# VectorE normalises all eight first tiles, GpSimd issues the weights between its powers, and the first and last attention chunk score their band units ahead of the products

## The reference

```
x = x + LN(attention(LN(x)))        # Wq, Wk, Wv 1024x1024 with biases, 16 heads of 64
x = x + LN(ffn(LN(x)))              # silu(x Wg') * (x Wu'), then Wd'; hidden 3072, int weights / 127
```

## Time and profile before

| | before |
|---|---|
| median of 3 runs | 1608.07 us (the fastest 1606.91) |
| the profiled execution | 1608.83 us, span of its slowest core 1607.8 us |
| spans of the 8 cores | 1602.8 to 1607.8 us |
| TensorE busy | 1551.7 us, 97% of the span |
| VectorE, ScalarE, GpSimd busy | 46%, 28%, 18% |
| chain that ended last | TensorE 94% |
| 0 to 10, 10 to 20, 20 to 30, 30 to 40, 40 to 50 us: TensorE busy | 0, 1.0, 2.5, 5.4, 7.7 us |
| 86 to 150 us (chunk 0): TensorE busy | 61.8 of 64 us |
| 562 to 640 us (most of chunk 7, and the FFN's start): TensorE busy | 70.5 of 78 us |
| 680 to 1608 us (FFN): TensorE busy | 920.5 of 928 us |

### The profile page before, as it was taken

How to read it: one execution, slowest core, us unless ns; L and a number is a source line. 1 busy time by engine, 2 the same in 40 slices (tenths; PEclk the granted TensorE clock), 3 DMA queues, 4 the chain that set the end, 5 groups by cost and what they waited for, 6 DMA issues and landing times.

```text
span 1607.8 us, 26300 instructions; the slowest of 8 cores (1602.8 to 1607.8 us)
## 1 busy us (share of the span) xinstructions
PE 1551.7 (97%) x9440; PEld 768.7 (48%) x9440; DVE 734.5 (46%) x1329; ACT 455.6 (28%) x566; POOL 293.8 (18%) x804
## 2 busy tenths in 40 slices
PE   2999999999999989999999999999999999999998
PEld 1455555555555554444444444444444444444443
DVE  3166555757565546424434434434434434433113
ACT  2445555555555551101111111111111111111111
POOL 3023323334332343200000001001001001001000
PEclk9999999999999999999999999999999999999999
DMA  9446756697664486932332333323322332322002
GB/s 222 92 76 129 144 101 119 139 155 151 135 114 97 91 243 220 246 110 85 92 99 98 92 86 111 93 85 111 88 77 97 85 95 92 92 79 95 10 1 92
DMA packets 130496, 178.41 MB, mean 111 GB/s; under 512 B 65472, under 2 KB 97216, under 8 KB 128960
## 3 DMA queue, kind: packets, MB, share of 16 engines
q1 hardware_dynamic: 110912, 99.11, 25.0%
q0 software_dynamic: 19024, 77.08, 19.4%
q10 hardware_dynamic: 432, 0.53, 0.1%
HBM read 136.85 MB, written 69.21 MB: 128 GB/s over the span
## 4 chain that ended last, share of the span: by engine, by line
PE 94%; DVE 1%; issue 1%; ACT 1%; POOL 1%; DMA 1%; DVEq 0%; POOLq 0%; SPq 0%; ACTq 0%
PE ps L655 21%; PE ps L665 21%; PE ps L721 20%; PE ps L293 14%; PE ps L323 7%; PE ps L368 4%; PE ps L394 3%; PE ps L391 2%; PE ps L418 1%; PE ps L440 1%; PE ps L623 1%; DMA xst<-x_in 0%; ACT pb L374 0%; DMA wdb_d<-wdT 0%; PE ps L263 0%
## 5 line engine op out<-in xcount | busy, mean ns | idle before, releaser
L655 PE MATMUL ps<-x2T,wg_sb 128*128 128x512 bf16 x1536 | 362.8, 379 | 1.2 <-DVE gacc L427 1.2
L665 PE MATMUL ps<-x2T,wu_sb 128*128 128x512 bf16 x1536 | 362.9, 379 | 0.0
L721 PE MATMUL ps<-wd_sb,hsw 128*128 128x512 bf16 x1488 | 322.5, 379 | 0.0
L374 ACT ACTIVATE pb<-ps 128x1024 bf16<-128x1024 f32 (+2 forms) x256 | 243.2, 1005 | 244.1 <-PE ps L368 244.1
L671 DVE TENSOR_TENSOR hsw<-ps,sgb 128x512 bf16<-128x512 f32 x192 | 132.8, 692 | 310.6 <-PE ps L665 310.6
L669 ACT ACTIVATE sgb<-ps 128x512 bf16<-128x512 f32 x192 | 114.6, 597 | 509.1 <-PE ps L655 497.4
L655 PEld LDWEIGHTS ps<-x2T,wg_sb 128*128 128x128 bf16 x1536 | 150.2, 98 | 181.9 <-issue 1.3
L665 PEld LDWEIGHTS ps<-x2T,wu_sb 128*128 128x128 bf16 x1536 | 150.2, 98 | 180.8
L721 PEld LDWEIGHTS ps<-wd_sb,hsw 128*128 128x128 bf16 x1488 | 145.6, 98 | 175.6
L172 POOL TENSOR_TENSOR small<-small 128x1 f32<-128x1 f32 x127 | 74.6, 588 | 742.6 <-DVE small L170 737.1
L381 POOL MEMSET pb<- 64x128 bf16 x488 | 111.7, 229 | 309.7 <-ACT pb L374 250.0
(11 more groups left out here) (80 smaller groups left out, 1093.4 us busy)
## 6 DMA issues: line engine op xcount, KB each, us to landing
xx<-x_in SPq DMA_DIRECT2D x34, 512.0 KB, 6.1
attn<-attn_d SPq DMA_DIRECT2D x32, 512.0 KB, 4.8
x_d<-xx POOLq DMA_DIRECT2D x32, 512.0 KB, 7.4
x1r<-x_d SPq DMA_DIRECT2D x32, 512.0 KB, 3.3
out<-x1r POOLq DMA_DIRECT2D x31, 512.0 KB, 3.0
xst<-x_in SPq DMA_DIRECT2D x29, 512.0 KB, 5.0
attn_d<-ast SPq DMA_DIRECT2D x58, 256.0 KB, 3.9
wgb_d<-wgT POOLq DMA_DIRECT2D x24, 256.0 KB, 5.7
```

Of the source, the lines that this page charges most:

```text
L374: s_free[buf] = tok["p", c, u, i] = AC.sig(ac.activation(pu[:, :, lo:hi], sp.rearrange("p (h e) -> p h e", h=2)[:, :, lo:hi], AF.Exp))
L655: mm = te.matmul(gp[:, p2], wg_sb[:, hc * 1024 + dc * 128:hc * 1024 + (dc + 1) * 128], xTn[:, dc * 512:(dc + 1) * 512], start=(dc == 0), s ...
L665: mm = te.matmul(upp[:, p2], wu_sb[:, hc * 1024 + dc * 128:hc * 1024 + (dc + 1) * 128], xTn[:, dc * 512:(dc + 1) * 512], start=(dc == 0), ...
L721: mm = te.matmul(ys[:, half * 512:(half + 1) * 512], hsw[:, hc * 512 + tt * 128:hc * 512 + (tt + 1) * 128], wd_sb[:, hc * DM + half * 512: ...
```

## The change

1. In the first eight tiles, every tile is normalised by VectorE; ScalarE's part (L237, L239) is gone.
2. The weight transfers no longer stand in front of all powers on GpSimd. Powers and transfers alternate by the table `w_turn`; the first transfer waits for the third tile of x, where it waited for the second before.
3. VectorE no longer waits for the biases ahead of the first statistics: the scaling of `bqs` stands behind the loop.
4. ScalarE runs one small exponential at the beginning, ahead of its first copy.
5. `k_group(0, 0)` stands behind the transposes of tile 3, one tile earlier; five groups of chunk 0 stand in the loop instead of four.
6. In chunks 0 and 7, except in the last slot, units 2 and 3 are scored right behind `q_group`, ahead of `ctx_out` and `pv`.
7. In the last slot `rot_n` is made even, so that `ctx_out` takes bank 0 and `pv_g` bank 1.

The diff, cut to its core:

```diff
-    PO.need(tok["x", 1])
...
-    for i in range(4):
+    def wk_load(i):
         w_load("wk", d_wk, wk_sb, wk_d, i)
...
-    DV.need(t_small)
-    tok["bqs"] = DV.sig(dv.tensor_scalar(bqs, bqs, QSCALE, None, ALU.mult))
+    AC.need(tok["mhalf"])
+    ac.activation(sc_(0, 3), mhalf, AF.Exp)
...
     def ln1_b(t):
-        k = 3 + t % 2
-        xn_t = xn[:, (t % 2) * DM:(t % 2 + 1) * DM]
-        if t < 8 and t % 2:
-            DV.need(tok["r0", t])
-            AC.need(DV.sig(dv.scalar_tensor_tensor(sc_(k, 2), mv_(k)[:, 0:1], -1.0, sc_(k, 1),
-                                                   ALU.mult, ALU.mult)), tok.get(("xTr", t - 2)))
-            tok["xn", t] = AC.sig(ac.activation(xn_t, x_at(t), AF.Identity, bias=sc_(k, 2),
-                                                scale=sc_(k, 1)))
-        else:
-            DV.need(tok["r0", t], tok.get(("xTr", t - 2)))
-            tok["xn", t] = normalise(k, xn_t, x_at(t))
+        DV.need(tok["r0", t], tok.get(("xTr", t - 2)))
+        tok["xn", t] = normalise(3 + t % 2, xn[:, (t % 2) * DM:(t % 2 + 1) * DM], x_at(t))
...
+    w_turn = {1: ((wk_load, 0), (wk_load, 1)), 2: ((wk_load, 2), (wk_load, 3)), 3: ((wv_load, 0),),
+              4: ((wv_load, 1),), 5: ((wq_load, 0), (wq_load, 1)), 6: ((wq_load, 2), (wq_load, 3))}
     for t in range(9):
         if t < 8:
             ln1_a(t)
+        if t == 1:
+            PO.need(tok["x", 2])
+        for load, i in w_turn.get(t, ()):
+            load(i)
         if t >= 1:
             ln1_b(t - 1)
             xT_pe(t - 1)
-        if t >= 5:
-            k_group(0, t - 5)
-    for u in range(4):
+        if t >= 4:
+            k_group(0, t - 4)
+    DV.need(t_small)
+    tok["bqs"] = DV.sig(dv.tensor_scalar(bqs, bqs, QSCALE, None, ALU.mult))
+    for u in range(5):
         k_group(1, u)
     for c in (0, 1):
-        for u in range(4, NU):
+        for u in range(5, NU):
             k_group(c, u)
...
+        few = c in (0, NCH - 1) and n + 1 < len(slots)
...
             q_group(*slots[n + 1])
+        else:
+            rot_n[0] += rot_n[0] % 2
+        if few:
+            band_scores()
         if n >= 2:
             ctx_out(*slots[n - 2])
         if n >= 1:
             pv(*slots[n - 1])
-        scores(c, u, 2, 0)
-        scores(c, u, 3, 1)
+        if not few:
+            band_scores()
```

More of the change, by code:

```diff
@@ L212, in w_load, with wq_load, wv_load @@
             w_d[2 * i:2 * i + 2].rearrange("u p e -> p u e")))
-    for i in range(4):
+    def wk_load(i):
         w_load("wk", d_wk, wk_sb, wk_d, i)
-    for n in range(2):
+    def wq_load(i):
+        w_load("wq", d_wq, wq_sb, wq_d, i)
+    def wv_load(n):
         tok["wv", n] = d_wv[n].sig(po.dma_start(wv_sb[:, n * 4096:(n + 1) * 4096], wv_d[n]))
-    for i in range(4):
-        w_load("wq", d_wq, wq_sb, wq_d, i)
     d_small.sig(ac.dma_start(bqs, bq_d))
@@ L553, in build_nc, with band_scores @@
             PO.need(tok["cast"], tok["k", 7, 7], tok["vmm", 7], tok["qmm", 6], tok["xT", NT - 1])
+        def band_scores():
+            scores(c, u, 2, 0)
+            scores(c, u, 3, 1)
         scores(c, u, 0, 0)
         scores(c, u, 1, 1)
+        few = c in (0, NCH - 1) and n + 1 < len(slots)
         if more and c > 0:
```

## The result

The changed kernel takes 1589.59 us (median of 5 runs, 1588.82 to 1592.4), against 1608.07 before: a ratio of 0.9888, with a 95% interval of 0.9873 to 0.9904. That is 18.5 us less; 28.3 were forecast. 1580.5 was said, with a range of 1574 to 1590: the result lies at the range's upper end, and a third of the forecast gain is missing. That it still lies inside is luck: the range reached to 1590 for rival C (1589), which didn't happen; what filled it were rivals A and B in part, and a wait that no rival held. Runs in which one die's cores showed a lower clock are left out of all ratios and means here.

A forecast was written before the change was run, and what follows sets the result against it. TensorE, busy 97% of the span, was taken as the bound, so edits pay only where it waits. From 1608.8 us, 16.7 for the start and 11.55 for the attention's end were subtracted: 1580.5, range 1574 to 1590.

The forecast's parts named there:

- rival C: Chunk 7: slots stay near 6.1 us, only the last bank and last slot pay, 1589 us; chance 0.09.
- rival A: Start: wk pair 0 lands 4.5 us later, first k group at 27.2, total 1585 us; chance 0.14.
- Rival B: Slot 57: the clock falls after the longer stall, half clock costs 2 to 2.5 us, 1583 us; chance 0.12.
- The time of the tiles: Start: tile 0 normalised at 11.2 us, then 2.80 us per tile; first k group can start at 22.7, against 33.57.
- The weights: Start: wk pair 0 issued at about 12.4, lands at 22.1, 0.6 us to spare; no wait for weights.
- Chunk 0: New unit order in chunk 0: between 0.1 us lost per slot and 2.2 us gained; taken as 0.
- Chunk 7's slots: Chunk 7, slots 57 to 62: 1.28 us of stall goes from each, 6.14 us becomes 4.86.
- the last interval: Chunk 7, `pv` of slot 61 to slot 62: 2.5 us of work, but masks end later; taken as 2.9 us.
- the other bank: Last slot: `gate(0)` takes the other bank, ending a 1.21 us wait for `pv_g`'s; part of a 3.05 us gain.
- the attention's end: End of chunk 7 up to `gate(0)`: 8.8 + 3.05 + 0.15 - 0.45 = 11.55 us gained.
- the masks of slot 63: Last slot: `pv` meets its masks too early by about 0.45 us, since TensorE comes sooner.
- The rule on the clock: TensorE, slot 57: by the skill page an idle stretch drops it to half rate; the trace showed both outcomes, unsettled.

The follow-up runs named there:

- third_store_buffer: The changed kernel with three staging buffers instead of two for the attention's output in chunk 7: median 1585.8 us, ratio 0.9855.
- attention_only: The kernel before with the new attention order and the turn of `rot_n`, on the old start: median 1608.4 us, ratio 0.9987.
- first_weight_early: The changed kernel with wk's first transfer moved ahead of the second tile's statistics, waiting for the second tile of x, not the third: ratio 0.9884.

## Why the forecast was wrong

**The time of the tiles** was right. VectorE's period was 2.80 us, the first tile was normalised at 12.0 (11.2 forecast, with tile 1 of x 0.9 us later on this core), and the full clock came some 5 us after unbroken work began, as taken: the group at 29.47 still took 2.22 us, the next one 1.89. On core 5, the one forecast from, the k groups end at 56.1.

**The weights** were the rival A of the forecast, and it came in part. wk took 11.3 us instead of 9.7 and was issued at 13.4, not 12.4. Of the 2.6 us missing at the first group 1.7 are the wait for wk and 0.9 the late tile 1; 0.8 are won back by the end of the groups, 1.8 stay. This landing differs from core to core (the quickest of the four transfers took 8.5 to 11.9 us): four of the eight cores had no wait for wk, and the slowest had one.

**Chunk 0** was forecast as nothing. From one q group to the next its slots take 6.2 to 6.8 us in both kernels, in all 0.3 us more than before. Behind it TensorE waits for a transposing DMA on two of the eight cores; on the slowest this wait of 1.8 us costs 1.3 against before. By slot 56 about 1.0 us has been won back, in small pieces that I didn't trace; 0.7 us in all are missing.

**Chunk 7's slots** were right: 4.96 for 4.86 us. Around them two terms were mis-sized. Rival B happened on three cores: the wait for the masks of slot 56 rose to 2.5 us on the slowest core (2.6 forecast) and the clock fell for some 4 us behind it (0.89, then 0.76 of full): the interval to the next `pv` (547.65 to 554.17) took 6.5 us instead of 4.86, which is 1.7 of the 2.8 us. And the last interval took 3.5 us instead of 2.9, in part since `ctx_out` waits 0.8 us for a bank; the masks of the slot end at 577.05, later than taken, and would have held `pv` to about 577.2 anyway (an estimate). The turn of `rot_n`, which frees `gate(0)`, puts `ctx_out` behind `pv_g` on bank 0. I had written of "the other bank" and only followed `gate(0)`.

**The step that failed** is the sum of the attention's end, which was too large by 7.6 us (2.8 up to `gate(0)`, 4.8 behind it): "8.8 + 3.05 + 0.15 - 0.45 = 11.55", closed by "The FFN weights are loaded ahead of their use by far more than this". The weights are in time. What I didn't price are the stores of the attention that run beside them. The same transfers now fall into shorter slots: the DMA engines' share of 0.76 in slots of 6.14 us becomes 0.86 in slots of 4.96, and the norm's loads (1 MB) are issued 3.9 us ahead of the store (571.51 to 575.43), where they were 5.2 ahead of it (589.13 to 594.31). A store that took 6.7 us took 10.9. With two staging buffers the store of slot 60 must land before the output of slot 62 is written. It had 11.1 us for this; now it has 7.5, since the last interval and `gate(0)` come sooner too. VectorE waits for the store; behind it in its queue stands the copy to `ctxT`, and `up(0)` waits for that. It costs 2.3 us on the slowest core (2.3 to 4.3 on the eight), plus the half clock behind it (0.83 in 586 to 592 us), which six of the eight cores show. With the third buffer `gate(0)` to `gate(2)` takes 10.4 to 10.6 us on all cores, where it is 14.7 on this one: 4.1 of the 4.8 us are the store, which is shown. The other 0.7 is the masks of slot 63, for which 0.45 us had been taken and 0.15 won back in `gate(0)`: even with the third buffer this stretch is 1.0 us longer than before. On most cores it shows as a wait of 0.8 us of `pv` for the masks, on the slowest as a hole of 0.75 us in the middle of `gate(0)`, without a releaser, behind which `pv` meets the masks just in time (582.80 against their end at 582.65).

**The rule on the clock.** That page of the Trainium skill, "TensorE: Matmul & The Clock Gate", section "What's actually happening", says that an idle stretch drops the engine to half rate. The runs bear it out only in part. At the masks of slot 56 the changed kernel looks orderly: waits up to 1.6 us left the granted clock at 1.00, waits of 2.5 us and more were followed by 0.50 to 0.89. But at `up(0)` two of its cores waited 2.75 and 2.96 us and kept 1.00, and in the other runs a wait of 1.84 us at the masks was followed by 0.50 (core 7 of third_store_buffer) and one of 2.98 us left 1.00 (core 1 of first_weight_early). So the length of a wait doesn't settle by itself whether the clock falls, and no run here shows what does. Removing the wait removed the drop.

**Slowest and mean.** The forecast was made on one core. The mean of the cores gained 19.5 to 20.4 us, the slowest about 18.5; the difference of 1 to 2 us is hardly larger than the 0.9 us between the chips, and in the profiled executions alone the mean gained 18.4. What the change brought differs from core to core: DMA landings in three places.

## What to carry to other kernels

When a stretch is made shorter, list every transfer that is issued in it and ask how long each may take until its buffer is needed again, counted in the new order and not in the trace of before. Two buffers that were enough with 11.1 us from a store's issue to the next use of its buffer weren't with 7.5, and the wait showed on an instruction three steps further on. Where cores differ by when DMA lands, a change that trades a fixed wait for a DMA wait can gain less on the slowest core than on the mean: attention_only gained 2 us there and 3.6 on the mean.

## What the runs showed of the hardware

With FFN weights, stores and two loads of 512 KB issued in slots of 4.96 us, the slowest store of 256 KB in chunk 7 took 10.9 to 12.9 us on the eight cores of the changed kernel; in slots of 6.14 us, with the same loads, 6.1 to 7.2; in slots of 4.96 us without the two loads, 5.7 to 7.3. A transposing DMA of one tile, 7.9 us in one trace, took 17.8 on one core of another, where two more landed in 12.1 and 7.4 us (the first on the same core, the second on core 5). Behind waits of 2.3 to 4.3 us at one and the same instruction the granted clock fell to 0.50 on some cores and stayed at 1.00 on others. The row of a wait can name an engine whose work ends at that moment though a DMA was waited for: one core of eight named TensorE for the 5.82 us of VectorE, the other seven named the store.
